# Attention slots for the row maxima: packed by columns and put in a new order

## The reference

```python
qkv = hidden_states @ Wqkv
q = qkv[..., :nH * d].reshape(B, S, nH, d)
k = qkv[..., nH * d:nH * d + d]
v = qkv[..., nH * d + d:]
scores = jnp.einsum('bqhd,bkd->bhqk', q, k) * scale
alibi = slopes[:, None, None] * (pos_k - pos_q).astype(jnp.float32)
scores = jnp.where(causal[None, None], scores + alibi[None], NEG_INF)
probs = jax.nn.softmax(scores, axis=-1)
attn = jnp.einsum('bhqk,bkd->bqhd', probs, v).reshape(B, S, H)
x = x + attn @ Wo
```

## Time and profile before

| | us |
|---|---|
| median of three runs (703.44 to 704.35) | 703.57 |
| the profiled execution | 700.96 |
| its span in the trace | 699.2 |
| slot pipeline: from the first slot matmul to the last copy of a turn | 32.3 to 523.5 |

### The profile page before, as it was taken

How to read it: one execution, slowest core, us unless ns; L and a number is a source line. 1 busy time by engine, 2 the same in 40 slices (tenths; PEclk the granted TensorE clock), 3 DMA queues, 4 the chain that set the end, 5 groups by cost and what they waited for, 6 DMA issues and landing times.

```text
span 699.2 us, 13261 instructions
## 1 busy us (share of the span) xinstructions
PE 669.7 (96%) x4304; PEld 305.5 (44%) x4304; DVE 557.4 (80%) x1801; ACT 358.6 (51%) x511; POOL 216.9 (31%) x366
## 2 busy tenths in 40 slices
PE   3889999999999999999999999999999999999997
PEld 2434344544344444444443343433433455555553
DVE  5899889887989889898988989899881365666565
ACT  2324647567556676666666666767667411111111
POOL 0035424233332515243352231422432412222220
PEclk9999999999999999999999999999999999999999
DMA  8578108080411443080144744225200189700001
GB/s 253 130 145 137 64 2 136 30 147 28 166 54 51 60 89 108 11 131 34 41 63 94 102 81 77 49 49 94 48 18 33 52 130 170 162 30 30 31 30 60
DMA packets 42951, 56.32 MB, mean 81 GB/s; under 512 B 6648, under 2 KB 26232, under 8 KB 42752
## 3 DMA queue, kind: packets, MB, share of 16 engines
q1 hardware_dynamic: 40296, 51.27, 37.3%
q10 hardware_dynamic: 2592, 4.26, 1.8%
HBM read 35.72 MB, written 19.79 MB: 79 GB/s over the span
## 4 chain that ended last, share of the span: by engine, by line
PE 83%; DVE 10%; DMA 3%; ACT 2%; issue 1%; SPq 1%; POOL 0%; DVEq 0%; ACTq 0%; POOLq 0%
PE psum L780 20%; PE psum L732 18%; PE psum L762 13%; PE psum L808 8%; PE psum L830 7%; PE psum L678 7%; PE psum L759 5%; DVE psum L1145 3%; PE psum L825 2%; PE psum L840 2%; ACT work L965 2%; DMA x_sb<-in_x 1%; DVE negm L1150 1%; PE psum L817 1%; DMA arena<-q_dram 1%
## 5 line engine op out<-in xcount | busy, mean ns | idle before, releaser
L965 ACT ACTIVATE work<-psum 128x1024 f32<-128x1024 f32 (+1 forms) x320 | 289.0, 943 | 127.6 <-PE psum L762 108.5
L1145 DVE CUSTOM_DVE_ANT_0 psum<-psum,future 128x384 f32<-128x384 f32 (+3 forms) x512 | 237.7, 514 | 12.6 <-PE psum L732 10.4
L732 PE MATMUL psum<-k_op,arena 106*128 106x512 bf16 (+3 forms) x768 | 212.4, 328 | 9.6 <-DVE negm L1145 4.3
L1150 DVE TENSOR_REDUCE negm<-psum 128x1 f32<-128x512 f32 x256 | 168.6, 687 | 15.3 <-PE psum L732 10.9
L1318 POOL TENSOR_SCALAR_AFFINE_SELECT work<-work 128x512 f32<-128x512 f32 x128 | 81.2, 634 | 296.2 <-ACT work L965 296.2
L780 PE MATMUL psum<-work,v_op 128*32 128x512 f32 (+3 forms) x1536 | 163.5, 498 | 0.5 <-POOL work L1318 0.4
L762 PE MATMUL psum<-arena,k_op 109*128 109x512 bf16 (+3 forms) x640 | 157.3, 316 | 1.9 <-ACT work L965 0.8
L732 PEld LDWEIGHTS psum<-k_op,arena 106*128 106x128 bf16 x768 | 69.0, 97 | 128.5 <-DVE negm L1145 40.7
L678 PE MATMUL psum<-arena,wqkv_sb 128*128 128x256 f32 (+3 forms) x240 | 84.6, 453 | 1.1 <-ACT arena L887 1.1
L759 PE MATMUL psum<-arena,k_op 116*128 116x128 bf16 x512 | 84.3, 221 | 0.9 <-ACT work L965 0.9
L762 PEld LDWEIGHTS psum<-arena,k_op 109*128 109x128 bf16 x640 | 59.6, 98 | 44.5 <-ACT work L965 15.7
(11 more groups left out here) (86 smaller groups left out, 454.8 us busy)
## 6 DMA issues: line engine op xcount, KB each, us to landing
arena<-q_dram SPq DMA_DIRECT2D x96, 128.0 KB, 5.5
o_dram<-o_sb SPq DMA_DIRECT2D x32, 256.0 KB
q_dram<-arena SPq DMA_DIRECT2D x16, 384.0 KB, 4.4
arena<-o_dram SPq DMA_DIRECT2D x32, 128.0 KB, 4.6
arena<-rcp_dram SPq DMA_DIRECT2D x32, 128.0 KB, 4.9
out<-wqkv_sb ACTq DMA_DIRECT2D x16, 256.0 KB, 2.0
x_sb<-in_x SPq DMA_DIRECT2D x3, 1024.0 KB, 10.0
work<-in_x SPq DMA_DIRECT2D x3, 1024.0 KB, 18.8
```

Source lines behind the costliest of these rows:

```text
L732: last = nc.tensor.matmul(bank[:, a * width:(a + 1) * width], q_op[0:ROW_MAX, bass.ds(col, P)], k_op[0:ROW_MAX, b, k0:k0 + width], start=T ...
L965: nc.scalar.activation(probs[:, n % 4, heads * hp:heads * (hp + 1), 0:w], src, ACT.Exp).then_inc(exp_done, 1)
L1145: last = nc.vector.tensor_tensor_reduce(keys, keys, future[:, CH - width:CH], -1.0, 3e38, ALU.add, ALU.min, negm[:, late, 0, j * QT + t:j ...
L1150: nc.vector.tensor_reduce(dst, psum[:, bank, 0:len(js) * width].rearrange("p (a k) -> p a k", a=len(js)), AX_X, ALU.max, negate=True).then ...
```

## The change

max_slots builds other slots and puts them in another order. A slot's tuple now holds its parts, pairs of head j and tile t, in place of one t and several heads:

- "uneven": 384 columns of a head's tile 2 and 128 columns of its tile 0 in one bank, four slots of 512 columns
- "pairs": tile 1 of two heads as before, two slots of 512 columns
- "wide": tile 3, four slots of 512 columns

The early unit has 10 slots (uneven, pairs, wide), the late one 26: full tiles 0 and 1, pairs, full tile 2, uneven, full tile 3, wide. With the two turns NSL is 38 (42 before). The planner's vector_time is the sum over the parts (275, 375, 500, 700), so that the sum of a step is the same. PE and DVE walk through the parts with a running column; the increment of the semaphore is at the last part. A nop in front of the masked reductions, emitted only in a loop that the kernel does not use for the slots, goes too.

```diff
@@ max_slots
-    out = []
-    for t in range(QT):
-        if late:
-            out += [("full", late, t, (j,)) for j in range(UH)]
-        per = 2 if t < 2 else 1
-        out += [("diag", late, t, tuple(range(j, j + per))) for j in range(0, UH, per)]
-    return out
+    full = [[("full", late, ((j, t),)) for j in range(UH)] for t in range(QT)]
+    pairs = [("diag", late, ((j, 1), (j + 1, 1))) for j in range(0, UH, 2)]
+    uneven = [("diag", late, ((j, 2), (j, 0))) for j in range(UH)]
+    wide = [("diag", late, ((j, 3),)) for j in range(UH)]
+    if not late:
+        return uneven + pairs + wide
+    return full[0] + full[1] + pairs + full[2] + uneven + full[3] + wide
@@ vector_time
-    time = 450 if kind == "turn" else 680 if kind == "full" else (550, 750, 500, 700)[t]
+    time = 450 if kind == "turn" else 680 if kind == "full" else sum((275, 375, 500, 700)[t] for _, t in parts)
@@ max_slot
-                width = P * (t + 1) if kind == "diag" else CH
-                k0 = CH * late if kind == "diag" else 0
-                for a, j in enumerate(js):
+                k0, at = CH * late if kind == "diag" else 0, 0
+                for j, t in parts:
+                    width = P * (t + 1) if kind == "diag" else CH
                     col = unit_col(2 * k + late, j, None) + t * P
-                    last = nc.tensor.matmul(bank[:, a * width:(a + 1) * width], q_op[0:ROW_MAX, bass.ds(col, P)],
+                    last = nc.tensor.matmul(bank[:, at:at + width], q_op[0:ROW_MAX, bass.ds(col, P)],
                                             k_op[0:ROW_MAX, b, k0:k0 + width],
                                             start=True, stop=True)
+                    at += width
                 last.then_inc(slot_full, 1)
@@ step (vector)
-                        if i is not None:
-                            dve.nop(nofuse=True)
-                        for a, j in enumerate(js):
-                            keys = psum[:, bank, a * width:(a + 1) * width]
+                        at = 0
+                        for j, t in parts:
+                            width = P * (t + 1)
+                            keys = psum[:, bank, at:at + width]
                             last = nc.vector.tensor_tensor_reduce(keys, keys, future[:, CH - width:CH], -1.0, 3e38, ALU.add, ALU.min,
                                                                   negm[:, late, 0, j * QT + t:j * QT + t + 1])
+                            at += width
                         last.then_inc(slot_free, 1)
```

More of the change, by code:

```diff
@@ L106 @@
 TURN = [EARLY_SLOTS + TURN_AFTER, len(SLOTS) + 1]
-SLOTS.insert(TURN[0], ("turn", 0, None, None))
-SLOTS.insert(TURN[1], ("turn", 1, None, None))
+SLOTS.insert(TURN[0], ("turn", 0, None))
+SLOTS.insert(TURN[1], ("turn", 1, None))
 NSL = len(SLOTS)
@@ L165, in vector_time @@
 def vector_time(k, r):
-    kind, _, t, _ = SLOTS[r]
-    time = 450 if kind == "turn" else 680 if kind == "full" else (550, 750, 500, 700)[t]
+    kind, _, parts = SLOTS[r]
+    time = 450 if kind == "turn" else 680 if kind == "full" else sum((275, 375, 500, 700)[t] for _, t in parts)
     if r in KEY_SLOTS.get(k, ()):
@@ L703, in max_slot @@
             def max_slot(k, r):
-                kind, late, t, js = SLOTS[r]
+                kind, late, parts = SLOTS[r]
                 bank, before = SLOT_AT[k, r]
@@ L1136, in step @@
                     dve.wait_ge(slot_full, at_loop(idx + 1, i, 2 * NSL))
-                    width = P * (t + 1) if kind == "diag" else CH
-                    where = 1 if kind == "full" else 0
                     if kind == "diag":
-                        if i is not None:
-                            dve.nop(nofuse=True)
-                        for a, j in enumerate(js):
-                            keys = psum[:, bank, a * width:(a + 1) * width]
+                        at = 0
+                        for j, t in parts:
+                            width = P * (t + 1)
+                            keys = psum[:, bank, at:at + width]
                             last = nc.vector.tensor_tensor_reduce(keys, keys, future[:, CH - width:CH], -1.0, 3e38, ALU.add, ALU.min,
                                                                   negm[:, late, 0, j * QT + t:j * QT + t + 1])
+                            at += width
                         last.then_inc(slot_free, 1)
                         continue
-                    dst = negm[:, late, where, :].rearrange("p (j t) -> p j t", t=QT)[:, js[0]:js[-1] + 1, t]
-                    nc.vector.tensor_reduce(dst, psum[:, bank, 0:len(js) * width].rearrange("p (a k) -> p a k", a=len(js)),
-                                            AX_X, ALU.max, negate=True).then_inc(slot_free, 1)
+                    (j, t), = parts
+                    nc.vector.tensor_reduce(negm[:, late, 1, j * QT + t:j * QT + t + 1], psum[:, bank], AX_X, ALU.max, negate=True
+                                            ).then_inc(slot_free, 1)
             def reciprocals(b):
```

## The result

I forecast 700.6 us (697.3 to 704.2), faster. Measured: 704.32 us median of 22 runs (702.88 to 706.90), against 702.73 us of the kernel before in 22 runs beside them (700.62 to 704.35). The ratio is 1.0032 (1.0021 to 1.0042), which is also that of the means, 704.83 and 702.61 us; the two medians alone would give 1.0023. The changed kernel is slower by 0.2 to 0.4%: the sign was wrong, and the time lies just outside the range.

The account below looks back on a forecast made before the run. PE was taken as the bound, with little over 1 us of waiting in a 27.77 us step. Terms 0.6 + 0.5 + 0.9 + 0.9 + 0.1 = 3.0 us off 703.57 gave 700.6 us (697.3 to 704.2).

Parts of the forecast that it names:

- Step 0: First step, taken as bound by DVE with the same work: 0.1 us won, between -0.5 and +0.5.
- the cover: Step 0, second half's keys ready 1.3 us later: one 0.65 us slot of DVE work still covers PE's 0.5 us.
- Step 1: DVE's idle time ahead of the norms goes, 0.2 us of the DMA wait is hidden: 0.9 us, between 0 and 1.7.
- Steps 2 to 4: Three steps with key pieces: 0.2 us for each start plus 0.1 for the rest, 0.9 us, between -1 and +2.
- the 0.6 us that I had set beside the sum: Step 4's key piece, coming behind GpSimd's subtraction, wins back most of 0.85 us: sum about 3.6 us instead of 3.0.
- Steps 5 to 9: Side-work steps: +0.2 us at the start, +0.1 late, -0.2 at tile 6's scores: 0.1 us each, 0.5 in all.
- the term for the start: Steps 5 to 9: front wait gone, ACT's exponential issued later, -0.31 + 0.11, so tile 2's scores come 0.2 us sooner.
- Steps 10 to 15: Steps without side work: nothing at the start, 0.1 us each from the first late-half bank wait, 0.6 us in all.
- The wall: Steps without side work: PE waits for DVE's chain at the last early wide slot, so the start's 0.31 us wins 0.
- The start value: Time before the change, the median of three runs, 703.57 us, from which the 3.0 us were taken.
- (a): Rival, chance 0.28: waits only move everywhere, leaving 0.6 us and a few tenths: 702.7 us, within the noise.
- (b): Rival, chance 0.14: slower, ACT's exponentials fed later in steps 1 to 9, 0.21 us each time: about 706 us.

Follow-up runs that it names:

- the version with both lists moved: Changed kernel with step 0's key pieces behind slots 0 to 6 instead of 2 to 8 and its norms behind 12 to 15 instead of 14 to 17: 700.53 us, ratio 0.9974.

## Why the prediction was wrong, point by point

**The bound** held: steps 5 to 9 still exceed 10 to 15 by their side work, and removing waits of PE elsewhere shortened the steps.

**Step 0** is the step that failed: "DVE is the bound (30.05 busy of 32.00 us), with the same work: 0.1 us, between -0.5 and +0.5", and "No wait is added". The same list of instructions is not the same work where their neighbours change. I had weighed the pinned numbers for steps 1 to 4 and never asked what the norms of step 0, moved past the turn, would meet on GpSimd: 3.3 us of DVE time in the profile. I even had the price in hand. The rows of step 4 show a key piece at 1.44 us beside GpSimd's subtraction, and step 0 of the kernel before had such a piece too, its last one, at 1.60 us (43.77). In the changed kernel that one is clear at 0.74 us (47.13), and two others take 1.44 and 1.33 us. The section of the Trainium skill that I cited for step 4 (SBUF — State Buffer, Who interferes with whom) also says that copy, cast and tensor_scalar can contend with GpSimd when they run in a two-port mode. The norm is a tensor_scalar, and its times (0.55 us alone, up to 1.46 and in one run 1.76 beside a split) agree with that; in which mode it runs no run here shows. The second part was the cover: my claim that one slot of DVE work covers the 0.5 us from k_ready to a full slot came true (DVE waited 0.05 us at 48.60), but I looked at the covered engine alone. PE stood 2.77 us, and its clock fell; the price came 3 us later, as DVE's 1.27 and 1.47 us.

**The sum for steps 1 to 15** was 2.9 us; 3.1 came (3.2 against the profile the prediction rested on). That it came so close is luck in part: steps 5 to 9 gave 0.4 us less than forecast and steps 10 to 15 0.5 us more. By parts:

- Step 1: 0.9 forecast, 0.8 measured (34.17 to 33.36). DVE's idle time ahead of the norms went, as said. And the wait of tile 4's scores for the DMA went altogether, not by 0.2 us. In the version with both lists moved it is back and step 1 takes 33.8 us:

```profile
78.90 0.60 PE L764 MATMUL psum<-arena,k_op 109*128 109x512 bf16 x2 [0.77 <-DMA arena<-m_dram]
```

  So half of the 0.8 us hangs on where the norms of step 0 stand. The wait is gone in the three packed versions that have them behind the turn (33.4 us each) and 0.8 to 1.2 us long in the five that have them at slots 12 to 15 (33.6 to 34.1 us). The length of step 0 doesn't decide it: it lasted 35.8 us with the splits held back, where the wait is gone, and 36.9 us with the norms alone moved, where it is there. What does, these runs do not show; where the wait stands, SP stores the maxima 4.2 us after the copy of turn 1 (74.64 and 70.46, both lists moved), and in the changed kernel 2.6 us after it (78.19 and 75.61).
- Steps 2 to 4: 0.9 forecast, 1.2 measured, nearly all of it in step 4 (32.90 to 31.66 us), whose key piece now misses GpSimd's splits (184.73 to 187.98). What had cost 1.44 us and 0.85 us of PE in the earlier trace rows is this after the change:

```profile
187.06 0.39 PE L733 MATMUL psum<-k_op,arena 106*128 106x512 bf16 x1 [0.36 <-DVE negm L1150]
...
188.75 0.68 DVE L1110 TENSOR_TENSOR k_tmp<-k_tmp 96x512 bf16<-96x512 f32 x1
```

  That is the 0.6 us that I had set beside the sum, by the Trainium skill's rule, and had not built on: I should have. The 0.2 us for each start did not come in steps 2 and 3 (+0.06 and -0.03 us).
- Steps 5 to 9: 0.1 us each forecast, 0.01 measured. The mechanism was right (the wait at the start goes, ACT's gate takes its place), and the term for the start was mis-sized, by a slip in the sum. Four slots of 512 columns instead of three are 0.22 us more by the forecast's own price, not 0.11, so tile 2's scores had to come 0.31 - 0.22 = 0.09 us sooner, not 0.20. They came 0.11 us sooner after the turn's copy (4.22 us against 4.33), and with 0.1 in place of 0.2 the parts add up to 0. PE waits there, and the weight load ahead of tile 6's scores (the last row) is held as long as before, 0.33 us:

```profile
273.69 0.10 PEld L761 LDWEIGHTS psum<-arena,k_op 116*128 116x128 bf16 x1 [0.42 <-ACT work L967]
273.69 0.23 PE L761 MATMUL psum<-arena,k_op 116*128 116x128 bf16 x1 [0.19 <-ACT work L967]
...
284.13 0.11 PEld L764 LDWEIGHTS psum<-arena,k_op 109*128 109x128 bf16 x2 [0.33 <-ACT work L967]
```

- Steps 10 to 15: 0.6 us forecast, 1.1 measured (0.1 in step 10, 0.2 in each of the others). Rows of step 13:

```profile
446.33 0.28 DVE L1136 COPY m_t<-psum 16x128 f32<-16x128 f32 x1 [1.35 <-PE psum L714]
...
447.90 0.11 PEld L733 LDWEIGHTS psum<-k_op,arena 106*128 106x128 bf16 x2 [0.41 <-DVE negm L1144]
...
451.94 0.10 PEld L733 LDWEIGHTS psum<-k_op,arena 106*128 106x128 bf16 x1 [0.55 <-DVE negm L1144]
451.95 0.39 PE L733 MATMUL psum<-k_op,arena 106*128 106x512 bf16 x1 [0.26 <-DVE negm L1144]
...
468.82 0.10 PEld L733 LDWEIGHTS psum<-k_op,arena 106*128 106x128 bf16 x1 [0.50 <-DVE negm L1150]
```

  The turn's copy no longer releases a weight load; the wait is stood out at the last wide slot, which holds a load for 0.55 us and not the 0.8 I had said, since part of the 0.31 is stood out ahead of it, behind ACT. The wall itself is where it was, 5.61 us after the turn's copy against 5.58, so the start won nothing, as forecast. The second wait of the late half stays at 0.50 us and the first is gone, worth 0.11 us as I had said. The other 0.08 us was won sooner in the late half, where in the kernel before a load of scores stood 0.43 us for ACT (at 453.07) and now none does; that stretch I had at nothing.

**The start value.** I hung the sum on the median of three runs, 703.57 us; over 22 runs it is 702.73. With that the forecast would have been 699.7 us, so the miss is 0.8 us larger than it looks.

**The rivals.** (a) had the right thing to say of steps 5 to 9, (b) the right sign with the wrong mechanism, since nothing was lost to ACT; none had step 0. The failure is not in a chance but in a case left out.

## What to carry to other kernels

When a change renumbers the slots under a list of pinned work, go through every entry of the list in every step, the first one too, and read what the *other* engines run at the new place: a norm on DVE beside a GpSimd subtraction took up to some three times its own duration here. "DVE is the bound and its work is the same" is a statement on durations, and they hold only as long as its neighbours do. And where a cover is said to hold, look at the engine that stands still under it, since PE came back at half its clock here after a wait of 2.77 us.

## What the runs showed of the hardware

- A norm (128x512 fp32 from SBUF to SBUF) takes 0.52 to 0.55 us alone and 0.77 to 1.76 us where it met a split's subtraction of some 1.15 us, by how much of the subtraction was still to come; an instruction on 128x4 elements went from 0.15 to 1.30 us. In two pairs in the rows above DVE's record ends behind GpSimd's although it began first: the small one began 0.13 us sooner (and ended at 55.41, the subtraction at 55.39), the norm at 53.34 began 0.32 us sooner (and ended at 55.10, the subtraction at 54.81).
- The clock fell to 1.2 GHz in step 0 at PE waits of 2.77 us (changed kernel), 2.31 us (keys later) and 1.74 us (both lists moved), for 6.8, 3.4 and 3.4 us: in the first two before the wait was over, in the third about 1 us behind it. After the same 2.77 us, with the splits held back, it fell 1.3 us behind the wait and for 3.4 us. In the second profile of before, with waits of 0.75 and 0.88 us, it stayed at 2.4 GHz. Runs of one kernel differ here: of 35 runs of the kernel before in one comparison 14 had a mean clock of 1.00 (mean 701.95 us) and 17 one of 0.997 (702.90 us).
- The start of the kernel scatters by more than the change is worth: the first reduction came between 32.6 and 36.1 us in thirteen profiles. Between two of them, 33.2 and 35.6 us, most of the difference is DVE's wait for the input's transfers, 6.0 and 7.8 us in all.
